# Attention and mixture-of-experts block in fp32: four buffer pairs for pair 1's rotation, and another order of batch 1's preparation

## The chip, the cores and the metric

The kernel runs on one core of a Trainium2 chip. The core has TensorE (PE) for matrix products, VectorE (DVE), ScalarE (ACT) and GpSimd (POOL) for the work on elements, SyncE (SP) to issue most DMAs, an on-chip memory (SBUF) and eight accumulation banks of 128 x 512 fp32 (PSUM), which GpSimd cannot reach. Each engine runs its own instructions in program order and waits on semaphores for the others. The metric is the device time of one launch in microseconds; the median of a few runs counts.

## The reference

The block has two batches of 1024 tokens with 128 features. Modulations (shift, scale, gate, twice) come from a small product. Then attention with 16 heads of 64, with latents of 64 for queries and for keys and values, and a mixture of 8 experts with the two best of each token:

```python
h = _layernorm(x) * (1 + ca) + sa
# inside the attention: a second layer norm with ln_scale, ln_bias
c_q, c_kv = h @ w_down_q.T, h @ w_down_kv.T        # 64 latents each
q, k, v = c_q @ w_up_q.T, c_kv @ w_up_k.T, c_kv @ w_up_v.T
q, k = rope(q), rope(k)                            # rotation by cos and sin
out = softmax(q @ k.T * scale) @ v @ w_out.T + residual
x = x + ga * out
h = _layernorm(x) * (1 + cb) + sb
x = x + gb * moe(h)        # where(weight > 0, relu(h*w @ w1 + b1) @ w2 + b2, out)
```

The attention scores are computed to nearly full fp32 from a rounded upper part (`_hi`) and a remainder (`_lo`) of q and k.

## The kernel before, in words

The work on attention goes by pairs of heads: 8 pairs in each batch, 16 in all, pair 0 to 7 for batch 0. A pair needs its up projections (`up`, q and k with a swapped twin for the rotation), their rotation, their upper and lower parts, the maxima of the scores' rows (16 steps, `maxima` on TensorE and `reduce_max` on VectorE), and then the main loop's 16 score steps with exponentials (ScalarE), values times probabilities (`pv`) and sums of probabilities (`add`, GpSimd). The main loop runs over p = 0 to 15 and 8 groups g of two score steps; beside pair p's scores, group g holds two maxima of pair p+1 and one of the eight units of pair p+2's up projections. So when the loop begins, pair 0 must be complete with maxima, pair 1 rotated, and batch 0 in latents. This is the prologue, where the change lies.

In the prologue, TensorE does batch 0's transposes and latents, `up(0, 0)` to `up(0, 3)`, `up(1, 0)` and `up(1, 1)`, and then the 16 maxima of pair 0. Between them stand `up(1, 2)` and `up(1, 3)`, batch 1's transposes (`transposed(2)`, `transposed(3)`: four tiles each), its latents (`latent(4)` to `latent(7)`) and its values (`values(1)`). Maxima use two pairs of banks in turn, so `maxima(0, n)` waits until the reduction of step n - 2 is done (`max_reduced` at n - 1). The first maxima of pair 1, `maxima(1, 0)`, open the main loop: they wait for all 16 reductions of pair 0.

Pair 1 is rotated on GpSimd: ScalarE copies a unit and its swapped twin out of PSUM (`up_copy(u)`, L727 and L728) to a buffer pair `turn_a`, `turn_b`; GpSimd multiplies both and adds (`turn_1`, L914 to L917); ScalarE writes the upper part (`upper_1`, L734), and GpSimd the lower part (`lower_1`, L923). There are two buffer pairs, so `up_copy(2)` waits for `lower_1(0)` and `up_copy(3)` for `lower_1(1)`.

Batch 1's first steps run along the same engines: ScalarE normalises x (`normalised(h0, x_sb, 0)`, L654, 8 tiles) once VectorE's `inverse(T1, 3)` has given the shifts (L1035); GpSimd modulates (`modulate`, L892, 2 instructions), and stands in front of `turn_1(0)`; VectorE takes the statistics (in program order behind `reduce_max(0, 1)`) and the inverse root (behind `reduce_max(0, 3)`, `shift` at L1035); ScalarE normalises again into `hn`; TensorE transposes, ScalarE scales (`features`, L672), TensorE computes the latents (L377), and ScalarE reads them (`latent_upper`, L680 and L682). GpSimd's last instructions of the prologue are `split(2)` (up weights), `lower_1(3)`, `gated(0)` (L871) and `residual(0, 0)` (L879). The first `add` follows.

SyncE issues eight small DMAs for each half of pair 0's maxima (`max_rows`) once `neg_max` is done; `score(0, 0)` waits for the first half's. The first exponential has a table load before it (L702). After the loop come the last outputs and the experts' products, with gathers and scatters by slots.

Of the kernel before, what the change touches and what calls it, by code (L numbers as in the profile page):

```python
# [10 lines left out]
F32 = mybir.dt.float32  # L11
# [10 lines left out]
HALF = 512  # L22
# [24 lines left out]
def build(nc, t, out):  # L47
    ctx = ExitStack()
    with ctx:
# [10 lines left out]
        x_sb = sb("x_sb", [P, NT, D])  # L60
        h0 = sb("h0", [P, NT, D])
# [58 lines left out]
        turn_a = [hid_sb[:, n, :] for n in range(2)]  # L120
        turn_b = [h2T[:, n * HALF:(n + 1) * HALF] for n in range(2)]
# [224 lines left out]
        def _(pe):  # L346
# [146 lines left out]
            for n in range(NMAX):  # L493
                maxima(0, n)
                if n == 1:
                    up(1, 2)
                    up(1, 3)
                if n == 4:
                    pe.wait_ge(s["up_copied"], 3)
                    transposed(2)  # L500
                    transposed(3)
                if n == 6:
                    pe.wait_ge(s["features"], 4)
                    latent(4)
                    latent(5)
                if n == 8:
                    pe.wait_ge(s["up_copied"], 4)
                    latent(6)
                    latent(7)
                if n == 11:  # L510
                    pe.wait_ge(s["latent_copied"], 2)
                    values(1)
# [121 lines left out]
        def _(act):  # L634
# [86 lines left out]
            def up_copy(u):  # L721

                act.wait_ge(s["up_product"], n_unit(1, u))
                if u >= 2:
                    act.wait_ge(s["pool_lower"], u - 1)
                straight, swapped = unit_banks(1, u)
                nc.scalar.copy(turn_a[u % 2], straight)  # L727
                nc.scalar.copy(turn_b[u % 2], swapped).then_inc(s["up_copied"], 1)  # L728

            def upper_1(u):  # L730
# [3 lines left out]
                nc.scalar.copy(hi_of[w][:, 1, c], turn_a[u % 2]).then_inc(s["pool_upper"], 1)  # L734

            root(3)
            values_out(0)
# [3 lines left out]
            normalised(h0, x_sb, 0).then_inc(s["norm1"], 1)  # L741
# [3 lines left out]
            upper(0, 3)  # L745
            upper_1(0)
            upper_1(1)
            up_copy(2)
            root(4)
            normalised(hn, h0, 1)  # L750
            features(2)
            features(3)
            up_copy(3)
# [75 lines left out]
        def _(pool):  # L829
# [77 lines left out]
            def turn_1(u):  # L907

                w, c = unit_columns(1, u)
                a, b = turn_a[u % 2], turn_b[u % 2]  # L910
# [8 lines left out]
            def lower_1(u):  # L919
# [3 lines left out]
                V.tensor_tensor(lo_of[w][:, 1, c], turn_a[u % 2], hi_of[w][:, 1, c].bitcast(F32),  # L923
# [640 lines left out]
```

## Time and profile before

| | |
|---|---|
| median of 3 runs | 905.26 us (905.06 to 907.29) |
| the profiled execution | 913.83 us |
| its span in the trace | 911.8 us |
| TensorE matmul busy | 818.4 us (90%) |
| GpSimd busy | 663.3 us (73%) |
| VectorE busy | 636.7 us (70%) |
| ScalarE busy | 396.9 us (44%) |
| mean granted TensorE clock | 0.948 |

Times in the trace are microseconds from the span's start. The prologue ends, and the main loop begins, with the first maxima that are written to `ps_m`, at 73.69 us. A row of a timeline merges equal instructions that follow one another: the second number is the time from the first's start to the last's end, and the count of matmuls is higher than that of the program's instructions, since an fp32 product is made in more than one pass. In brackets stands the idle time before, with the engine that ended it. The granted clock is 1.00 at 2.4 GHz and 0.50 at 1.2 GHz.

### The profile page before, as it was taken

How to read it: one execution, taken by the hardware profiler on the slowest of the kernel's cores; microseconds unless marked ns; L12 is line 12 of the kernel's file. 1: busy time of each engine (PE TensorE's matmuls, PEld its weight loads, DVE VectorE, ACT ScalarE, POOL GpSimd, SP SyncE). 2: the span in 40 equal slices, each digit the busy share in tenths (PEclk: the TensorE clock that was granted, in tenths of full speed). 3: DMA queues.
4: the chain of work that ended last, by engine and by line, in shares of the span. 5: the costliest groups of instructions: out<-in, count | busy, mean ns of one | idle time of the engine just before them, and what ended most of it. 6: DMA issues, size and time to landing. Idle time of an engine off the chain costs nothing.

```text
span 911.8 us, 14689 instructions
## 1 busy us (share of the span) xinstructions
PE 818.4 (90%) x5118; PEld 490.1 (54%) x5118; DVE 636.7 (70%) x1156; ACT 396.9 (44%) x650; POOL 663.3 (73%) x348
## 2 busy tenths in 40 slices
PE   4668999999999999999999999999999977788671
PEld 2435555555555555555555555555555443377661
DVE  8957777777777777777777777777776757654112
ACT  3453544444444444444444444444444322345331
POOL 2386998989897878787878787878778845623323
PEclk8968999999999999999999999999999987979786
DMA  9000001010101010101011110101000000186763
GB/s 245 27 1 12 13 13 25 14 25 13 25 13 25 14 25 13 25 13 25 13 27 26 21 25 14 25 13 14 13 14 14 13 13 12 43 267 228 255 228 87
DMA packets 84329, 43.89 MB, mean 48 GB/s; under 512 B 57632, under 2 KB 73376, under 8 KB 84192
## 3 DMA queue, kind: packets, MB, share of 16 engines
q1 hardware_dynamic: 83232, 40.86, 17.6%
q0 software_dynamic: 1024, 2.10, 0.7%
q8 instruction: 41, 0.67, 0.3%
q14 instruction: 32, 0.26, 0.1%
HBM read 36.51 MB, written 6.16 MB: 47 GB/s over the span
## 4 chain that ended last, share of the span: by engine, by line
PE 80%; DVE 8%; issue 4%; POOL 3%; DMA 3%; ACT 1%; SPq 1%; another core or an unknown queue 0%; POOLq 0%; DVEq 0%; ACTq 0%
PE ps_o L456 25%; PE ps_m L422 9%; PE ps_x L410 8%; PE ps_s L440 7%; PE ps_s L446 6%; PE ps_s L442 6%; PE ps_s L444 6%; PE ps_s L473 3%; PE ps_s L464 3%; PE ps_s L591 2%; DMA moe<-xs_dram 2%; PE ps_s L600 1%; DVE mx L1104 1%; POOL xs_dram L960 1%; DVE hn L1193 1%
## 5 line engine op out<-in xcount | busy, mean ns | idle before, releaser
L946 POOL TENSOR_TENSOR acc<-acc,probs 128x1024 f32<-128x1024 f32 (+1 forms) x192 | 459.8, 2395 | 76.2 <-ACT probs L702 53.8
L1104 DVE TENSOR_REDUCE mx<-ps_m 128x2 f32<-128x1024 f32 x240 | 293.7, 1224 | 93.1 <-PE ps_m L422 92.6
L702 ACT ACTIVATE probs<-ps_s 128x1024 f32<-128x1024 f32 x256 | 248.9, 1024 | 163.2 <-PE ps_s L446 163.1
L456 PE MATMUL ps_o<-probs,c_all 128*64 128x512 f32 x1024 | 250.4, 610 | 0.0
L946 POOL TENSOR_TENSOR acc<-probs 128x1024 f32<-128x1024 f32 (+1 forms) x32 | 75.4, 2358 | 54.8 <-ACT probs L702 54.3
L440 PE MATMUL ps_s<-q_hi,k_hi 64*128 64x512 f32 x512 | 103.4, 400 | 12.0 <-DVE x_sb L1160 10.9
L456 PEld LDWEIGHTS ps_o<-probs,c_all 128*64 128x64 f32 x1024 | 62.6, 137 | 93.9 <-issue 44.6
L422 PE MATMUL ps_m<-k_hi,q_hi 64*128 64x512 f32 x480 | 108.0, 445 | 3.9 <-DVE mx L1104 3.9
L442 PE MATMUL ps_s<-q_hi,k_lo 64*128 64x512 f32 x512 | 101.8, 393 | 0.0
L446 PE MATMUL ps_s<-neg_row,one_row 64*128 64x512 f32 x512 | 101.7, 393 | 0.0
L444 PE MATMUL ps_s<-q_lo,k_hi 64*128 64x512 f32 x512 | 101.1, 391 | 0.0
L422 PEld LDWEIGHTS ps_m<-k_hi,q_hi 64*128 64x128 f32 x480 | 46.2, 184 | 90.8 <-issue 80.4
L440 PEld LDWEIGHTS ps_s<-q_hi,k_hi 64*128 64x128 f32 x512 | 49.0, 187 | 24.4 <-issue 17.2
L1160 DVE TENSOR_TENSOR x_sb<-x_sb,ps_s 128x512 f32<-128x512 f32 x30 | 20.6, 686 | 49.9 <-PE ps_s L473 49.9
L444 PEld LDWEIGHTS ps_s<-q_lo,k_hi 64*128 64x128 f32 x512 | 48.9, 187 | 11.1
L442 PEld LDWEIGHTS ps_s<-q_hi,k_lo 64*128 64x128 f32 x512 | 49.1, 187 | 10.7
L446 PEld LDWEIGHTS ps_s<-neg_row,one_row 64*128 64x128 f32 x512 | 48.8, 186 | 10.9
L714 ACT COPY den<-ps_s 128x512 f32<-128x512 f32 x30 | 17.6, 585 | 78.0 <-PE ps_s L464 78.0
L1091 DVE TENSOR_TENSOR ps_x<-ps_x,tmp 128x256 f32<-128x256 f32 x112 | 48.4, 432 | 3.8
L694 ACT CAST q_hi<-ps_x 128x256 fp32r<-128x256 f32 x56 | 20.9, 374 | 66.6 <-DVE ps_x L1091 66.6
L1086 DVE TENSOR_TENSOR ps_x<-ps_x,rot 128x256 f32<-128x256 f32 x112 | 47.3, 422 | 0.0
L1089 DVE TENSOR_TENSOR tmp<-ps_x,rot 128x256 f32<-128x256 f32 (+1 forms) x113 | 47.0, 416 | 0.0
(289 smaller groups left out, 1030.5 us busy)
## 6 DMA issues: line engine op xcount, KB each, us to landing
probs<-in_experts SPq DMA_DIRECT2D x15, 578.0 KB
rr<-rd_dram SPq DMA_DIRECT2D x62, 128.0 KB
wu<-in_wqk SPq DMA_DIRECT2D x16, 256.0 KB, 3.2
neg_row<-nm SPq DMA_DIRECT2D x256, 0.5 KB, 2.0
w_first<-in_experts SPq DMA_DIRECT2D x5, 578.0 KB
rot<-in_experts SPq DMA_DIRECT2D x5, 578.0 KB
hT<-in_experts SPq DMA_DIRECT2D x5, 578.0 KB
xs_dram<-zero SPq DMA_DIRECT2D x2, 960.0 KB, 7.4
```

The lines of the kernel that those rows point to most:

```text
L410: ins = nc.tensor.matmul(bank, m[:, q % 2, w, twin, :], src, start=(n == 0), stop=(n == 1))
L422: ins = nc.tensor.matmul(bank[:, h, :], q_hi[rows(h), q % 3, qt * P:(qt + 1) * P], k_hi[rows(h), q % 3, kh * HALF:(kh + 1) * HALF], start= ...
L440: nc.tensor.matmul(bank[h], k_hi[rows(h), p % 3, kc], q_hi[rows(h), p % 3, qc], start=True, stop=False)
L442: nc.tensor.matmul(bank[h], k_lo[rows(h), p % 3, kc], q_hi[rows(h), p % 3, qc], start=False, stop=False)
L444: nc.tensor.matmul(bank[h], k_hi[rows(h), p % 3, kc], q_lo[rows(h), p % 3, qc], start=False, stop=False)
L446: ins = nc.tensor.matmul(bank[h], one_row[rows(h), :], neg_row[rows(h), p % 2, qc], start=False, stop=True)
L456: ins = nc.tensor.matmul(ps_o[64 * h:64 * h + 64, :], c_all[:, (p // HP) * TB + kt, :], probs[:, st % 4, h, :], start=(kt == 0), stop=(kt ...
L702: nc.scalar.activation(probs[:, st % 4, :, :], ps_s[:, 2 * (st % 2):2 * (st % 2) + 2, :], ACT.Exp, scale=SCALE).then_inc(s["probs"], 1)
L946: V.tensor_tensor(acc[:, half, heads, :], first, probs[:, st % 4, heads, :], ALU.add).then_inc(s["added"], 1)
L1086: V.tensor_tensor(straight, straight, cos_sb[:, c], ALU.mult).then_inc(s["turned"], 1)
L1091: V.tensor_tensor(straight, straight, part, ALU.add).then_inc(s["rotated"], 1)
L1104: V.reduce_max(mx[:, :, kh, qt], max_banks(q, n), AX.X).then_inc(s["max_reduced"], 1)
```

## The change

It has three parts. First, `turn_a` and `turn_b` get two more members each, in `rr` and in the second half of `acc`, and each unit of pair 1 has its own buffer pair; the wait of `up_copy` on `pool_lower` is gone. Second, ScalarE's order: the first normalisation of batch 1 stands ahead of `values_out(0)`, `up_copy(2)` and `up_copy(3)` follow `upper(0, 3)`, and `upper_1(1)` stands behind the second normalisation. Third, TensorE's order between the maxima: `transposed(2)` and `transposed(3)` go behind steps 6 and 7 instead of both behind step 4; the four latents go one by one behind steps 9 to 12 instead of two by two behind steps 6 and 8; `values(1)` goes behind step 14 instead of 11. No instruction is added or taken away on any engine.

```diff
--- before.py
+++ after.py
@@ -117,8 +117,8 @@
         wo_sb = p_flat[0:64, 0:H * D].rearrange("p (h d) -> p h d", h=H)
         g_tmp, g_abs = [probs[:, 2 + n, 0, :].rearrange("p (b m d) -> p b m d", b=B, m=2) for n in range(2)]
         g_raw = w_first[:, 0:HP * D]
-        turn_a = [hid_sb[:, n, :] for n in range(2)]
-        turn_b = [h2T[:, n * HALF:(n + 1) * HALF] for n in range(2)]
+        turn_a = [hid_sb[:, n, :] for n in range(2)] + [rr[:, 0, :], acc[:, 1, 0, :]]
+        turn_b = [h2T[:, n * HALF:(n + 1) * HALF] for n in range(2)] + [rr[:, 1, :], acc[:, 1, 1, :]]
 
         latent_raw = [moe[:].rearrange("p a d -> p (a d)")[64:128, n * HALF:(n + 1) * HALF] for n in range(3)]
         latent_raw.append(rt_sb[:].rearrange("p a d -> p (a d)")[64:128, 0:HALF])
@@ -495,19 +495,14 @@
                 if n == 1:
                     up(1, 2)
                     up(1, 3)
-                if n == 4:
+                if n in (6, 7):
                     pe.wait_ge(s["up_copied"], 3)
-                    transposed(2)
-                    transposed(3)
-                if n == 6:
+                    transposed(n - 4)
+                if n >= 9 and n < 13:
                     pe.wait_ge(s["features"], 4)
-                    latent(4)
-                    latent(5)
-                if n == 8:
                     pe.wait_ge(s["up_copied"], 4)
-                    latent(6)
-                    latent(7)
-                if n == 11:
+                    latent(n - 5)
+                if n == 14:
                     pe.wait_ge(s["latent_copied"], 2)
                     values(1)
             pe.wait_ge(s["values"], 2)
@@ -721,36 +716,34 @@
             def up_copy(u):
 
                 act.wait_ge(s["up_product"], n_unit(1, u))
-                if u >= 2:
-                    act.wait_ge(s["pool_lower"], u - 1)
                 straight, swapped = unit_banks(1, u)
-                nc.scalar.copy(turn_a[u % 2], straight)
-                nc.scalar.copy(turn_b[u % 2], swapped).then_inc(s["up_copied"], 1)
+                nc.scalar.copy(turn_a[u], straight)
+                nc.scalar.copy(turn_b[u], swapped).then_inc(s["up_copied"], 1)
 
             def upper_1(u):
 
                 w, c = unit_columns(1, u)
                 act.wait_ge(s["pool_rotated"], u + 1)
-                nc.scalar.copy(hi_of[w][:, 1, c], turn_a[u % 2]).then_inc(s["pool_upper"], 1)
+                nc.scalar.copy(hi_of[w][:, 1, c], turn_a[u]).then_inc(s["pool_upper"], 1)
 
             root(3)
+            normalised(h0, x_sb, 0).then_inc(s["norm1"], 1)
             values_out(0)
             folded_out()
             upper(0, 0)
             upper(0, 1)
-            normalised(h0, x_sb, 0).then_inc(s["norm1"], 1)
             up_copy(0)
             upper(0, 2)
             up_copy(1)
             upper(0, 3)
+            up_copy(2)
+            up_copy(3)
             upper_1(0)
-            upper_1(1)
-            up_copy(2)
             root(4)
             normalised(hn, h0, 1)
+            upper_1(1)
             features(2)
             features(3)
-            up_copy(3)
             upper_1(2)
             for n in range(4, 8):
                 latent_upper(n)
@@ -907,7 +900,7 @@
             def turn_1(u):
 
                 w, c = unit_columns(1, u)
-                a, b = turn_a[u % 2], turn_b[u % 2]
+                a, b = turn_a[u], turn_b[u]
                 if u == 0:
                     pool.wait_ge(rot_in, 32)
                 pool.wait_ge(s["up_copied"], u + 1)
@@ -920,7 +913,7 @@
 
                 w, c = unit_columns(1, u)
                 pool.wait_ge(s["pool_upper"], u + 1)
-                V.tensor_tensor(lo_of[w][:, 1, c], turn_a[u % 2], hi_of[w][:, 1, c].bitcast(F32),
+                V.tensor_tensor(lo_of[w][:, 1, c], turn_a[u], hi_of[w][:, 1, c].bitcast(F32),
                                 ALU.subtract).then_inc(s["pool_lower"], 1)
 
             turn_1(0)
```

On TensorE, the rows from behind `up(1, 3)` to batch 1's values stand as follows before (L422 are the maxima, L370 the transposes, L377 the latents, L384 the values):

```order
L422 MATMUL ps_s<-k_hi,q_hi 128x512 x6
L370 MATMUL ps_m<-ident,hn 128x128 x8
L422 MATMUL ps_s<-k_hi,q_hi 128x512 x4
L377 MATMUL ps_m<-hT,wd_sb 128x512 x2
L422 MATMUL ps_s<-k_hi,q_hi 128x512 x4
L377 MATMUL ps_o<-hT,wd_sb 128x512
L377 MATMUL ps_x<-hT,wd_sb 128x512
L422 MATMUL ps_s<-k_hi,q_hi 128x512 x6
L384 MATMUL ps_m<-wd_sb,hT 128x64 x8
L422 MATMUL ps_s<-k_hi,q_hi 128x512 x8
```

and after the change, up to the last latent but not the two maxima and the values behind it:

```order
L422 MATMUL ps_s<-k_hi,q_hi 128x512 x10
L370 MATMUL ps_m<-ident,hn 128x128 x4
L422 MATMUL ps_s<-k_hi,q_hi 128x512 x2
L370 MATMUL ps_m<-ident,hn 128x128 x4
L422 MATMUL ps_s<-k_hi,q_hi 128x512 x4
L377 MATMUL ps_m<-hT,wd_sb 128x512
L422 MATMUL ps_s<-k_hi,q_hi 128x512 x2
L377 MATMUL ps_m<-hT,wd_sb 128x512
L422 MATMUL ps_s<-k_hi,q_hi 128x512 x2
L377 MATMUL ps_o<-hT,wd_sb 128x512
L422 MATMUL ps_s<-k_hi,q_hi 128x512 x2
L377 MATMUL ps_x<-hT,wd_sb 128x512
```

Here the transposes are parted and later by two and three steps of maxima, and each latent has two matmuls of one maxima step on either side.

On ScalarE, from the root that opens batch 1's chain (`sd`), the rows stand as follows before (L654 `h0` is the first normalisation, L686 `values_out`, L666 `folded_out`, L694 the upper parts of pair 0, L727 and L728 `up_copy`):

```order
L642 ACTIVATE sd<-sd 128x8
L686 COPY c_all<-ps_m 128x512
L666 COPY w_first<-ps_m 128x512
L666 COPY w_first<-ps_o 128x512
L694 CAST k_hi<-ps_s 128x512
L694 CAST q_hi<-ps_s 128x512
L654 ACTIVATE h0<-x_sb,shift,sd 128x128 x8
L727 COPY hid_sb<-ps_s 128x512
L728 COPY h2T<-ps_s 128x512
L694 CAST k_hi<-ps_m 128x512
L727 COPY hid_sb<-ps_s 128x512
L728 COPY h2T<-ps_s 128x512
```

and after the change (the same instructions have line numbers lower by 5 to 7):

```order
L637 ACTIVATE sd<-sd 128x8
L649 ACTIVATE h0<-x_sb,shift,sd 128x128 x8
L681 COPY c_all<-ps_m 128x512
L661 COPY w_first<-ps_m 128x512
L661 COPY w_first<-ps_o 128x512
L689 CAST k_hi<-ps_s 128x512
L689 CAST q_hi<-ps_s 128x512
L720 COPY hid_sb<-ps_s 128x512
L721 COPY h2T<-ps_s 128x512
L689 CAST k_hi<-ps_m 128x512
L720 COPY hid_sb<-ps_s 128x512
L721 COPY h2T<-ps_s 128x512
```

The first normalisation has moved from behind `q_hi` of unit 1 to the place ahead of `c_all`; what followed it keeps its order.

Next on ScalarE, from the upper part of pair 0's last unit (L694 `q_hi<-ps_o`) to the upper part of pair 1's unit 2 (`k_hi`), the rows stand as follows before:

```order
L694 CAST q_hi<-ps_o 128x512
L734 CAST k_hi<-hid_sb 128x512
L734 CAST q_hi<-hid_sb 128x512
L727 COPY hid_sb<-ps_m 128x512
L728 COPY h2T<-ps_m 128x512
L642 ACTIVATE sd<-sd 128x8
L654 ACTIVATE hn<-h0,shift,sd 128x128 x8
L672 ACTIVATE hT<-ps_m,lns 128x512 x2
L727 COPY hid_sb<-ps_o 128x512
L728 COPY h2T<-ps_x 128x512
L734 CAST k_hi<-hid_sb 128x512
```

and after the change:

```order
L689 CAST q_hi<-ps_o 128x512
L720 COPY rr<-ps_m 128x512
L721 COPY rr<-ps_m 128x512
L720 COPY acc<-ps_o 128x512
L721 COPY acc<-ps_x 128x512
L727 CAST k_hi<-hid_sb 128x512
L637 ACTIVATE sd<-sd 128x8
L649 ACTIVATE hn<-h0,shift,sd 128x128 x8
L727 CAST q_hi<-hid_sb 128x512
L667 ACTIVATE hT<-ps_m,lns 128x512 x2
L727 CAST k_hi<-rr 128x512
```

The copies of units 2 and 3 now go to `rr` and `acc` ahead of the first `upper_1`, and `upper_1(1)` (`q_hi<-hid_sb`) comes behind the eight tiles of `hn`. GpSimd's order is unchanged.

## Rows read from the trace of the kernel before

**Rows 1.** The page's chain that ended last: share of the span by engine.
```profile
PE 80%; DVE 8%; issue 4%; POOL 3%; DMA 3%; ACT 1%; SPq 1%; another core or an unknown queue 0%; POOLq 0%; DVEq 0%; ACTq 0%
```
**Rows 2.** Busy time of each engine by window, inside the main loop.
```profile
200.00:400.00 200.00, 200.00 (x1270) 113.82 (x1270) 154.29 (x253) 93.06 (x128) 171.19 (x77) 1.00 0.10 19
```
**Rows 3.** Timeline of ScalarE: start, us, line, operation, count, idle before and releaser.
```profile
29.59 0.58 ACT L686 COPY c_all<-ps_m 128x512 f32<-128x512 f32 x1 [4.62 <-PE ps_m L384]
...
33.10 3.19 ACT L654 ACTIVATE h<-x_sb,shift,sd 128x128 f32<-128x128 f32 x8
...
36.66 0.59 ACT L728 COPY h2T<-ps_s 128x512 f32<-128x512 f32 x1
...
52.57 3.19 ACT L654 ACTIVATE hn<-h,shift,sd 128x128 f32<-128x128 f32 x8 [1.29 <-DVE shift L1035]
```
**Rows 4.** Timeline of GpSimd (POOL) in the prologue.
```profile
36.37 4.85 POOL L892 TENSOR_TENSOR h<-h,mod 128x1024 f32<-128x1024 f32 x2 [14.19 <-ACT h L654]
...
41.18 1.26 POOL L914 TENSOR_TENSOR hid_sb<-hid_sb,rot 128x512 f32<-128x512 f32 x1
...
48.75 1.26 POOL L923 TENSOR_TENSOR k_lo<-hid_sb,k_hi 128x512 fp32r<-128x512 f32 x1
...
51.25 1.26 POOL L914 TENSOR_TENSOR hid_sb<-hid_sb,rot 128x512 f32<-128x512 f32 x1 [1.24 <-ACT h2T L728]
...
70.08 2.35 POOL L879 TENSOR_TENSOR h<-h,mod 128x1024 f32<-128x1024 f32 x1
```
**Rows 5.** Timeline of VectorE (DVE) in the prologue.
```profile
25.86 0.17 DVE L1035 SCALAR_TENSOR_TENSOR shift<-mv,sd 128x8 f32<-128x8 f32 x1
...
39.81 2.35 DVE L1104 TENSOR_REDUCE mx<-ps_s 128x2 f32<-128x1024 f32 x2
...
44.95 2.34 DVE L1104 TENSOR_REDUCE mx<-ps_s 128x2 f32<-128x1024 f32 x2
...
51.55 0.99 DVE L1035 SCALAR_TENSOR_TENSOR shift<-mv,sd 128x8 f32<-128x8 f32 x1
...
68.93 4.62 DVE L1104 TENSOR_REDUCE mx<-ps_s 128x2 f32<-128x1024 f32 x4 [0.79 <-PE ps_s L422]
```
**Rows 6.** Timeline of TensorE (PE) from pair 1's projections to the loop's third group.
```profile
34.83 0.39 PE L410 MATMUL ps_s<-ck,wl 128*128 128x512 f32 x1
...
46.31 0.80 PE L422 MATMUL ps_s<-k_hi,q_hi 64*128 64x512 f32 x2 [3.51 <-DVE mx L1104]
...
53.21 3.07 PE L370 MATMUL ps_m<-ident,hn 128*128 128x128 f32 x8 [6.10 <-ACT hn L654]
...
56.22 1.22 PE L422 MATMUL ps_s<-k_hi,q_hi 64*128 64x512 f32 x4
...
57.37 3.78 PE L377 MATMUL ps_m<-hT,wd_sb 128*128 128x512 f32 x4
...
62.19 1.12 PE L377 MATMUL ps_o<-hT,wd_sb 128*128 128x512 f32 x2
...
66.45 2.00 PE L384 MATMUL ps_m<-wd_sb,hT 128*128 128x64 f32 x16
...
73.69 0.80 PE L422 MATMUL ps_m<-k_hi,q_hi 64*128 64x512 f32 x2 [1.76 <-DVE mx L1104]
...
84.95 0.50 PE L422 MATMUL ps_m<-k_hi,q_hi 64*128 64x512 f32 x2
```
**Rows 7.** Windows of 1 us with the granted clock (PEclk) where it changes.
```profile
45.00:46.00 1.00, 0.00 (x0) 0.00 (x0) 1.00 (x2) 0.62 (x1) 1.00 (x2) 0.51 0.00 0
...
62.00:63.00 1.00, 1.00 (x4) 0.49 (x3) 1.00 (x1) 0.37 (x1) 1.00 (x1) 0.95 0.00 0
...
72.00:73.00 1.00, 0.00 (x0) 0.00 (x0) 1.00 (x2) 0.00 (x0) 0.43 (x1) 0.67 0.00 0
...
79.00:80.00 1.00, 0.66 (x5) 0.48 (x5) 1.00 (x3) 0.00 (x0) 0.96 (x1) 0.92 0.08 1
```
**Rows 8.** Waits in the last 111 us: engine, line, releaser: us, times, longest.
```profile
ACT hid_sb L797 <- remote: 9.4, 2, 6.8
```

## The prediction

> **What bounds the kernel now.** I read the page's chain first: TensorE carries 80% of it [rows 1]. The windows say why: from 200 to 400 us TensorE is busy for 200.00 of 200.00 us, GpSimd for 171 and VectorE for 154 [rows 2]. In the loop TensorE's order is the limit, and none of its instructions changes there. So the question is when `maxima(1, 0)`, the loop's first instruction, starts: 73.69 us now, behind VectorE's last reduction of pair 0 [rows 6]. What the prologue gains there is carried to the end, as long as the loop has no slack to swallow it; with TensorE gapless it has none.
>
> Then the timelines of the prologue, engine by engine. The reader is to see a relay: ScalarE's first normalisation of batch 1 starts at 33.10, though its shifts were there at 26.03 [rows 3, 5]; ScalarE instead waited 4.62 us for `values_out` [rows 3]. GpSimd waits 14.19 us for it and modulates from 36.37 [rows 4]. `turn_1(0)` follows at 41.18, and `lower_1(0)` ends at 50.0; only then does `up_copy(2)` run, because it needs the buffer; behind it stand the root and the second normalisation, which starts at 52.57 [rows 3, 4]. VectorE had its statistics by 44.95 [rows 5]. TensorE waits 6.10 us for `hn` [rows 6], with the granted clock down to half speed since 45 us [rows 7], so that transposes, latents and maxima from 53.21 to 62 run at 1.2 GHz.
>
> **First half of the change: the start of the chain.** The normalisation now begins at 26.1 and takes 3.19 us, to 29.3. `values_out` was released at 29.59 [rows 3], so the gap of 4.62 us holds it and costs it nothing; the cover is thin, 0.3 us, and every 0.1 us above that would delay `values_out`, the folded weights and `up(0, 2)` by as much. GpSimd's two modulations (4.85 us, rows 4) run from 29.4 to 34.2. `up_copy(0)` no longer stands behind the normalisation, but it needs `up(1, 0)`, whose last matmul ends at 35.2 [rows 6]; its two copies end at 36.4, against 37.25 before [rows 3]. So `turn_1(0)` starts at 36.4 and not at 41.18: 4.8 us earlier. A `turn_1` is 3.8 us (41.18 to 44.97) and a `lower_1` 1.26 us [rows 4].
>
> The first maxima move little: `up(1, 1)` cannot be earlier, since it waits for VectorE. VectorE starts its first two reductions at 39.7, against 39.81 [rows 5], and the statistics end at 44.9 as now.
>
> **Four buffer pairs.** `up_copy(2)` and `up_copy(3)` run as their products appear, at 40.3 and 41.3, when ScalarE has nothing else to do. They cost the path nothing. What they buy is that the root and the second normalisation no longer stand behind `lower_1(0)`. What is late next is VectorE's order: reductions 2 and 3 stand in front of the inverse root and end at 47.2 [rows 5]. The root itself (ScalarE, 0.2 us) is done by 45.4. Then the inverse and the shift: 0.2 us, and 0.99 us for the shift beside a busy GpSimd, against 0.17 us for the same instruction with GpSimd idle [rows 5]. GpSimd will be busy at that time too (`turn_1(2)`), so I take 0.99. The normalisation then starts at 48.6 and ends at 51.8, against 52.57 and 55.76 [rows 3]: 4.0 us earlier.
>
> A page of the Trainium skill bears on this shift: "GPSIMD Engine Reference", section 1 (Specifications), says that GpSimd shares its SBUF interfaces with VectorE and that they contend when VectorE's instruction has two SBUF inputs or runs in a two-port mode. The row at 51.55 agrees and has the size that the page lacks. With the contention-free 0.17 us everything behind the shift would come 0.8 us sooner; the sum goes by the row.
>
> `upper_1(1)` now waits behind these eight tiles, to 52.3, so `lower_1(1)` on GpSimd starts at 52.4, though GpSimd was free at 49.0. Behind it: `turn_1(3)` to 57.4, `lower_1(2)` to 58.7, `split(2)` to 61.2. The added wait of about 3 us is GpSimd's alone, and I follow it below.
>
> **TensorE between the maxima.** `maxima(4)` and `maxima(5)` follow reductions 2 and 3, cold (0.80 us, rows 6). Reduction 4 runs from 48.5 to 49.7, behind the shift; `maxima(6)` from 49.8. From here TensorE has work without a gap. At 1.2 GHz a maxima step is 0.6 us (1.22 for two), four transposes 1.53 (3.07 for eight), a latent 1.87 (3.78 for two); at 2.4 GHz a maxima step is 0.45 and a latent 1.0 (1.12 with the rise inside it) [rows 6]. In order: maxima 6 to 50.4, transposes to 51.9, maxima 7 to 52.5, transposes to 54.0 (the last tile is ready at 51.8), maxima 8 and 9 to 55.2, latent 4 (features ready at 54.9) to 57.1, maxima 10 to 57.7, latent 5 to 59.5.
>
> When does the clock rise? Today TensorE's unbroken work begins at 53.21 and the rise comes at 62.05 [rows 6, 7], 8.8 us later and 5.8 us after the last transpose. The same two distances from 50.4 and 54.0 give 59.2 and 59.8; I take 59.5. Then maxima 11 to 60.0, latent 6 to 61.0, maxima 12 to 61.5, latent 7 to 62.5, maxima 13 and 14 to 63.5, values (2.00 us, rows 6) to 65.4, maxima 15 to 65.9, and its reduction to 67.2 (four take 4.62 us, rows 5; one alone 1.2). VectorE is not behind: its reductions 8 to 14 need 1.2 us each and each gets its banks 1.5 us or more apart, but for the last three, of which reduction 14 ends at 65.5. Moving the values from step 11 to 14 costs some 0.6 us here, since reduction 15 now waits for them; it is in the sum. The loop begins at 67.3 instead of 73.69: 6.4 us.
>
> Bounds for the unseen clock: if it stays at half speed through all pieces, latents 6 and 7 end at 62.0 and 64.5, the values at 67.6, and the loop begins at 69.6: 4.1 us. If it rises at 55.2, the loop begins at 65.4: 8.3 us.
>
> **The loop's first groups.** Today the clock falls again at 72.67, after 69.1 to 72.7 in which TensorE had only short maxima between four reductions [rows 5, 7], and the first groups run at 1.2 GHz to 79.1. Groups 0 and 1 take 11.26 us, 73.69 to 84.95 [rows 6]. In the new order latents and values fill the place in front of the loop, and the longest gap there is 1.4 us, the last reduction. I expect the clock to stay at 2.4 GHz. Then 5.4 us of cold work could shrink by 2.7 at the most; walking through groups 0 and 1, `maxima(1, 2)` and `maxima(1, 3)` still wait for reductions of 1.24 us and the two rotations on VectorE, and I get 9.2 us: 2.0 saved. The bounds are 0 and 2.7.
>
> **GpSimd at the loop's start.** Latent 7 is read by ScalarE to 63.8 (two copies of 0.58, as in rows 3), `upper_1(3)` to 64.4, `lower_1(3)` to 65.7, `gated(0)` to 68.1, `residual(0, 0)` (2.35 us, rows 4) to 70.4. The first `add` needs the probabilities of step 1, at 70.9 with a warm clock. So GpSimd is just in time, and its wait for `upper_1(1)` is covered; without this cover it would eat into a slack of (200 - 171)/200, about 0.7 us in each group of 5.03. The maximum rows leave SyncE at 53.9, land by 61, and are early. The table load of the exponential falls behind `values_out(1)`, from 66 to 67.3, ahead of its first use at 68.7.
>
> The sum: 6.4 + 2.0 = 8.4 us. The profiled execution would be 913.83 - 8.4 = 905.4 us, the median 905.26 - 8.4 = 896.9 us. The median runs stand 8.6 us below the profiled one; the gapless loop makes the prologue's gain the same in both, so I subtract and do not scale.
>
> **Rivals.** (a) The clock falls in front of the loop all the same, or has not risen long enough. For it: it fell at 45 about 2.2 us after the last matmul, and at 72.67 although work was scattered over the time before. Against: the gap is shorter and the work before it denser. Then 6.4 us alone: 898.9. (b) The clock stays low up to the loop: 4.1 us, 901.2. For it: there is one rise of this kind in the rows, and no other to tell how far it varies. (c) The clock rises early: 8.3 + 2.0 = 10.3 us, 894.9. (d) The head start is swallowed: GpSimd late by its chain `upper_1(1)`, `lower_1(1)` to `residual(0, 0)`, so that the exponentials wait for `add`. It would take back at most what GpSimd is late; from 70.4 to 78.6, 8 us of delay, nothing would be left: 905.3. Against: GpSimd has waited 3 us once and nothing else. (e) Slower: the experts' part at the end has waits that no instruction of the kernel ends, 9.4 us in two of them for ScalarE [rows 8]. If the code of an engine arrives late there, the time is lost on the path. The profiled execution, 8.6 us above the median, may be such a case. The changed program has the same instructions in other places; with 9.4 us more than today's median runs have, it would give 906.3. It decides from 8.4 us on. Against it: nothing in the change is near that part, and three runs lie within 2.3 us.
>
> **How the numbers follow.** The forecast has 0.58, (a) 0.18, (b) 0.06, (c) 0.10, (d) 0.04, (e) 0.04. The forecast's own range is 895.3 to 898.3, from 0.8 us for the shift and 0.7 us either way for the loop's first groups. The range of 8 in 10 goes from 894.2, below (c), to 901.3, which takes in (a) and (b). A change under 0.3% (2.7 us) can't be told from none. Faster means under 902.5: the forecast, (a), (b) and (c), with one hundredth off for a smaller sum: 0.91. The same: 0.05, (d) and that hundredth. Slower: 0.04.
>
> **What would show it.** In the profile after: ScalarE's `h` tiles end before 29.5 and `c_all` keeps its start at 29.6; GpSimd's modulation starts at 29.4, `turn_1(0)` at 36.4; `hn` starts at 48.6; the first `maxima` on `ps_m` is at 67.3; the granted clock rises near 59.5 and is 1.00 at 68 to 72; groups 0 and 1 last 9.2 us. The forecast is wrong if `hn` waits for something else than the shift, if the clock is 0.50 at the loop's start, if GpSimd's first `add` comes after the probabilities that it adds, or if TensorE shows gaps between 100 and 690 us that are not there now.

## The result, and the profile after

The changed kernel takes 897.46 us in the median of 5 runs (895.69 to 899.75), against 905.26 before: a ratio of 0.9908, 95% interval 0.9885 to 0.9930. The forecast was 896.9. A second series (below) gave 0.9925 (0.9898 to 0.9951). The profiled execution took 895.69 us with a span of 894.0.

ScalarE's timeline after (start, us, line, operation, count, idle before and releaser) answers to [rows 3]:

```profile
25.98 3.19 ACT L649 ACTIVATE h<-x_sb,shift,sd 128x128 f32<-128x128 f32 x8 [1.09 <-DVE shift L1028]
29.49 0.58 ACT L681 COPY c_all<-ps_m 128x512 f32<-128x512 f32 x1 [0.32 <-PE ps_m L384]
...
47.91 3.19 ACT L649 ACTIVATE hn<-h,shift,sd 128x128 f32<-128x128 f32 x8 [2.36 <-DVE shift L1028]
```

The first normalisation fills the gap, 0.32 us of it is left, and `c_all` keeps its start. `hn` starts at 47.91 (48.6 forecast) and is released by the shift.

GpSimd's timeline after answers to [rows 4]:

```profile
29.25 4.87 POOL L885 TENSOR_TENSOR h<-h,mod 128x1024 f32<-128x1024 f32 x2 [6.72 <-ACT h L649]
36.35 1.29 POOL L907 TENSOR_TENSOR hid_sb<-hid_sb,rot 128x512 f32<-128x512 f32 x1 [2.23 <-ACT h2T L721]
...
51.69 1.26 POOL L916 TENSOR_TENSOR q_lo<-hid_sb,q_hi 128x512 fp32r<-128x512 f32 x1 [2.62 <-ACT q_hi L727]
...
66.26 2.42 POOL L872 TENSOR_TENSOR h<-h,mod 128x1024 f32<-128x1024 f32 x1
68.83 2.39 POOL L939 TENSOR_TENSOR acc<-probs 128x1024 f32<-128x1024 f32 x1 [0.15 <-ACT probs L697]
```

`turn_1(0)` starts at 36.35, `lower_1(1)` has waited for `upper_1(1)`, and the first `add` comes 0.15 us after the residual's end, released by ScalarE: just in time, as worked out.

TensorE's timeline after answers to [rows 6]:

```profile
46.59 0.79 PE L422 MATMUL ps_s<-k_hi,q_hi 64*128 64x512 f32 x2 [4.17 <-DVE mx L1097]
47.72 0.80 PE L422 MATMUL ps_s<-k_hi,q_hi 64*128 64x512 f32 x2 [0.34 <-DVE mx L1097]
49.16 0.80 PE L422 MATMUL ps_s<-k_hi,q_hi 64*128 64x512 f32 x2 [0.65 <-DVE mx L1097]
49.89 1.11 PE L370 MATMUL ps_m<-ident,hn 128*128 128x128 f32 x4
...
53.87 2.07 PE L377 MATMUL ps_m<-hT,wd_sb 128*128 128x512 f32 x2
...
61.50 2.00 PE L384 MATMUL ps_m<-wd_sb,hT 128*128 128x64 f32 x16
63.43 0.50 PE L422 MATMUL ps_s<-k_hi,q_hi 64*128 64x512 f32 x2
65.35 0.50 PE L422 MATMUL ps_m<-k_hi,q_hi 64*128 64x512 f32 x2 [1.42 <-DVE mx L1097]
...
74.54 0.50 PE L422 MATMUL ps_m<-k_hi,q_hi 64*128 64x512 f32 x2
```

The 6.10 us wait for `hn` is gone; the loop starts at 65.35 instead of 73.69, and groups 0 and 1 take 9.19 us (74.54 - 65.35) instead of 11.26. The granted clock (third number from the right) rose early and did not fall again before the third group:

```profile
56.00:57.00 1.00, 1.00 (x3) 0.46 (x4) 0.29 (x1) 0.98 (x2) 1.00 (x2) 0.68 0.08 1
...
65.00:66.00 1.00, 0.65 (x6) 0.66 (x8) 0.49 (x3) 0.42 (x1) 1.00 (x1) 1.00 0.00 0
```

So in this pair of traces the third group starts 10.4 us earlier, more than the 8.4 forecast, while the medians moved 7.8.

### The profile page after: what moved, and what is told of

Its sections match the earlier page's. It is cut to its first block, busy times and chain, and to the rows that moved or that the text cites. A ratio compares the mean times of both kernels' runs of the same rounds, so it can differ in the third digit from the quotient of the medians.

```text
span 894.0 us, 14690 instructions
## 1 busy us (share of the span) xinstructions
PE 813.2 (91%) x5118; PEld 485.9 (54%) x5118; DVE 637.1 (71%) x1156; ACT 397.2 (44%) x650; POOL 662.7 (74%) x348
## 4 chain that ended last, share of the span: by engine, by line
PE 82%; DVE 8%; DMA 4%; POOL 2%; issue 2%; ACT 1%; POOLq 0%; SPq 0%; DVEq 0%
PE ps_o L456 25%; PE ps_m L422 9%; PE ps_x L410 8%; PE ps_s L440 7%; PE ps_s L442 6%; PE ps_s L446 6%; PE ps_s L444 6%; PE ps_s L473 3%; DMA moe<-xs_dram 3%; PE ps_s L464 3%; PE ps_s L595 2%; PE ps_s L586 2%; POOL xs_dram L953 2%; DVE mx L1097 1%; PE ps_s L377 1%
## 5 line engine op out<-in xcount | busy, mean ns | idle before, releaser
L422 PE MATMUL ps_m<-k_hi,q_hi 64*128 64x512 f32 x480 | 107.7, 444 | 4.0 <-DVE mx L1097 4.0
L939 POOL TENSOR_TENSOR acc<-probs 128x1024 f32<-128x1024 f32 (+1 forms) x32 | 75.4, 2357 | 48.3 <-ACT probs L697 47.8
L422 PEld LDWEIGHTS ps_m<-k_hi,q_hi 64*128 64x128 f32 x480 | 46.0, 183 | 91.4 <-issue 81.3
L440 PEld LDWEIGHTS ps_s<-q_hi,k_hi 64*128 64x128 f32 x512 | 48.7, 186 | 24.0 <-issue 17.0
L1153 DVE TENSOR_TENSOR x_sb<-x_sb,ps_s 128x512 f32<-128x512 f32 x30 | 20.6, 685 | 49.9 <-PE ps_s L473 49.9
L444 PEld LDWEIGHTS ps_s<-q_lo,k_hi 64*128 64x128 f32 x512 | 48.7, 186 | 10.8
L446 PEld LDWEIGHTS ps_s<-neg_row,one_row 64*128 64x128 f32 x512 | 48.6, 185 | 10.8
L442 PEld LDWEIGHTS ps_s<-q_hi,k_lo 64*128 64x128 f32 x512 | 48.7, 186 | 10.5
L709 ACT COPY den<-ps_s 128x512 f32<-128x512 f32 x30 | 17.6, 585 | 77.9 <-PE ps_s L464 77.9
```

The source lines that it names most:

```text
L422: ins = nc.tensor.matmul(bank[:, h, :], q_hi[rows(h), q % 3, qt * P:(qt + 1) * P], k_hi[rows(h), q % 3, kh * HALF:(kh + 1) * HALF], start= ...
L440: nc.tensor.matmul(bank[h], k_hi[rows(h), p % 3, kc], q_hi[rows(h), p % 3, qc], start=True, stop=False)
L442: nc.tensor.matmul(bank[h], k_lo[rows(h), p % 3, kc], q_hi[rows(h), p % 3, qc], start=False, stop=False)
L444: nc.tensor.matmul(bank[h], k_hi[rows(h), p % 3, kc], q_lo[rows(h), p % 3, qc], start=False, stop=False)
L446: ins = nc.tensor.matmul(bank[h], one_row[rows(h), :], neg_row[rows(h), p % 2, qc], start=False, stop=True)
L939: V.tensor_tensor(acc[:, half, heads, :], first, probs[:, st % 4, heads, :], ALU.add).then_inc(s["added"], 1)
```

## The experiments

Each row is one trace, with the median of its own series; the changed kernel has four traces. Since the traces are up to 1.9 us apart by the time of this step, I count from VectorE's first `shift` row (25.86 before, 25.78 after). The columns: start of ScalarE's `hn`, of the loop and of the third group (all from that shift), the clock in the first two groups ("low" is low at their start), the median and the ratio to the kernel before in the same series.

| kernel | `hn` | loop | third group | clock in groups 0, 1 | median us | ratio (95%) |
|---|---|---|---|---|---|---|
| before | 26.7 | 47.8 | 59.1 | low | 905.26 |  |
| before_again | 26.8 | 47.7 | 58.2 | low | 905.88 | 1.0006 (0.9995 to 1.0016) |
| changed | 22.1 | 39.6 | 48.8 | high | 897.46 | 0.9908 (0.9885 to 0.9930) |
| after_again | 21.0 | 38.4 | 47.6 | high | 899.20 | 0.9925 (0.9898 to 0.9951) |
| after_third | 21.0 | 38.5 | 47.7 | high | (894.55, one) |  |
| after_fourth | 23.6 | 40.1 | 50.9 | falls | (896.44, one) |  |
| pe_order_only | 26.8 | 45.6 | 54.8 | high | 902.79 | 0.9978 (0.9963 to 0.9994) |
| scalar_only | 22.2 | 43.4 | 54.0 | low | 902.62 | 0.9972 (0.9955 to 0.9989) |
| norm_late | 23.1 | 39.9 | 50.6 | falls | 898.01 | 0.9905 (0.9882 to 0.9928) |
| two_buffers | 22.2 | 41.2 | 50.4 | high | 897.42 | 0.9918 (0.9888 to 0.9948) |
| before_warm | 26.7 | 50.7 | 60.2 | rises at once | 907.14 | 1.0008 (0.9989 to 1.0026) |
| after_warm | 22.1 | 37.8 | 48.5 | falls | 897.96 | 0.9917 (0.9885 to 0.9949) |
| warm_all | 21.0 | 39.4 | 48.6 | high | 896.99 | 0.9899 (0.9883 to 0.9914) |
| warm_fit | 23.6 | 38.9 | 48.1 | high | 897.14 | 0.9894 (0.9873 to 0.9915) |

**The two kernels once more.** No edit.

> The kernel before once more, unchanged, for a second trace. Theory: the waits of ScalarE and VectorE in the experts' part that no instruction ends (about 17 us summed over the engines in the first trace, and none in the changed kernel's) are not a property of either kernel; here they are absent or elsewhere, and the profiled time is near 905. Rival: they belong to this kernel and come back, with a profiled time near 914, and then a part of the gain comes from the placement of code. The loop's start is at 73.7 us, within 1 us by either.

> The changed kernel once more, unchanged. Theory: the loop's start lies between 65 and 69.6 us, according to when TensorE's granted clock rises between 56 and 60 us, and the first two groups take 9.2 us; the rest of the spread sits in the experts' part. Rival: the loop's start is the same to 0.3 us each time and the whole spread comes from the experts' part. Median expected 897.5 us.

In `before_again` the profiled time is 904.02 us and the waits that no instruction ends [rows 8] are absent, so they belong to one execution and not to the kernel; rival (e) did not come. The changed kernel's loop start moved by 1.1 us (38.4 against 39.6), neither by 4 nor by 0.3, so both sides of that expectation were off. The 1.1 us is a small VectorE instruction: `sd<-mv` (L1021) took 1.29 us in the first trace and 0.17 in the second (last section). Over the four traces `hn` starts 21.0 to 23.6 us behind the first shift.

**TensorE's order alone; ScalarE's order and buffers alone.**

```diff
 # pe_order_only = before with the new placement between the maxima:
-                if n == 4: transposed(2), transposed(3)
-                if n == 6: latent(4), latent(5)
-                if n == 8: latent(6), latent(7)
-                if n == 11: values(1)
+                if n in (6, 7): transposed(n - 4)
+                if n >= 9 and n < 13: latent(n - 5)
+                if n == 14: values(1)
 # scalar_only = after with these lines the other way round
```

> The kernel before with TensorE's new order alone (transposes behind steps 6 and 7, latents behind 9 to 12, values behind 14). Theory: hn still starts at 52.6; from maxima 6 on it goes as in the changed kernel (49.2 to 65.4, 16.2 us), but from 53.6, so the loop starts at 69.8 and with a warm clock: 3.9 + 2.0 = 5.9 us gained, median about 899.4. Rival: the order only pays with the earlier hn; alone it costs what the values' move costs, and the gain is under 2 us (over 903).

> The changed kernel with TensorE's order of before: four buffer pairs and ScalarE's order alone. Theory: hn starts at 47.9, as in the changed kernel; the transposes then hold reductions 5 and 6, and the last four maxima run alone at the end, so the loop starts at 69.4 with the clock falling again: 4.3 us gained, median about 901.0. Rival: it is the earlier hn that brings the whole gain, and the order of TensorE nothing: 65.4 to 66 for the loop's start and 897 to 898 in the median.

In the medians the order alone gave 2.4 us, not 5.9; ScalarE's part alone 2.6, not 4.3. In `pe_order_only` maxima 6 started at 53.69, as expected, but the loop began at 71.32 instead of 69.8:

```profile
53.69 0.80 PE L422 MATMUL ps_s<-k_hi,q_hi 64*128 64x512 f32 x2 [5.60 <-DVE mx L1099]
...
59.17 2.04 PE L377 MATMUL ps_m<-hT,wd_sb 128*128 128x512 f32 x2 [0.71 <-issue]
...
61.87 1.85 PE L377 MATMUL ps_m<-hT,wd_sb 128*128 128x512 f32 x2
63.64 0.50 PE L422 MATMUL ps_s<-k_hi,q_hi 64*128 64x512 f32 x2
...
71.32 0.49 PE L422 MATMUL ps_m<-k_hi,q_hi 64*128 64x512 f32 x2 [1.42 <-DVE mx L1099]
```

From maxima 6 to the loop it takes 17.6 us, and not the 16.2 of the changed kernel. Two things make up the 1.4 us. Latent 4 stands still for 0.71 us until `up_copy(3)` has ended at 59.07, since this kernel has two buffer pairs and the changed kernel has no such wait. And the clock rose only at 63.4, so that latent 5 took 1.85 us instead of 1.13.

In `scalar_only` the loop starts where it was expected (43.4 from the shift, against 69.4 - 25.8 = 43.6). The clock falls at 61.1, during the values (59.96 to 62.64) and ahead of the last four maxima, and the groups cost 10.65 us.

The table shows which part gives what. ScalarE's part brings `hn` 4.6 us forward and leaves the way from `hn` to the third group as it was (31.9 us, against 32.4 and 31.4 before). The order leaves `hn` where it was and shortens this way to 28.1; with both it is 26.6, 26.6, 26.6 and 27.3. So the third group comes 3.8 and 4.6 us earlier with one part and 9.9 with both. That is nearly a sum: the 1.5 us above it is about what `pe_order_only` lost to the wait for `up_copy(3)` and the late rise. The medians say the same, 2.4 and 2.6 against 6.0 in the same series, and their intervals don't separate 5.0 from 6.0. Why these two medians gained 1.4 and 2.0 us less than their traces is open. The three moves within TensorE's order (transposes, latents, values) were not run apart.

**What brings `hn` forward.** `norm_late` moves the first normalisation back; `two_buffers` keeps it early and takes two of the four buffer pairs away.

```diff
 # norm_late
-            normalised(h0, x_sb, 0).then_inc(s["norm1"], 1)
             values_out(0)
...
             upper(0, 1)
+            normalised(h0, x_sb, 0).then_inc(s["norm1"], 1)
             up_copy(0)
 # two_buffers
-        turn_a = [...] + [rr[:, 0, :], acc[:, 1, 0, :]]      (and turn_b)
+                if u >= 2: act.wait_ge(s["pool_lower"], u - 1)
-            up_copy(2), up_copy(3), upper_1(0), root(4), normalised(hn, h0, 1), upper_1(1), features(2), features(3)
+            upper_1(0), upper_1(1), up_copy(2), root(4), normalised(hn, h0, 1), features(2), features(3), up_copy(3)
```

> The changed kernel with batch 1's first normalisation back behind upper(0, 1). Theory A (VectorE's order is the gate of hn): the statistics stand behind reduction 1 and end at 45 whether the modulation ends at 34 or at 41, so hn starts where it does in the changed kernel (47.9, within 0.5), and only GpSimd is 4.8 us later, which its waits cover to within 0.5 us at the first add: the loop starts at 65.4 (at the same clock) and the median is that of the changed kernel, 897.5 to 899.2. Theory B (the prediction's relay: ScalarE's early start is what brings the gain): hn at 51 to 52.6 and a median of 902 or more.

> The changed kernel with two buffer pairs, and ScalarE's order of before behind upper(0, 3), but with the early normalisation and TensorE's new order. Theory A: with GpSimd 4.8 us earlier, lower_1(0) ends at 45.3 and up_copy(2) at 46.3, so hn still starts at the shift, 47.9; up_copy(3) ends at 54.7 and holds latent 4 by 0.8 us at most; the loop starts at 65.4 to 66.2, median within 1 us of the changed kernel's. Theory B (the four buffers are needed): hn later than 50 and a median of 901 or more.

Theory A holds in both medians, 898.01 and 897.42; no difference from the changed kernel can be measured. The rows of VectorE, then ScalarE, of `norm_late` show it, though GpSimd's modulation ended 7 us later than in the changed kernel:

```profile
40.47 2.35 DVE L1097 TENSOR_REDUCE mx<-ps_s 128x2 f32<-128x1024 f32 x2
42.74 1.64 DVE L1015 BATCH_NORM_STATS2 bst<-h 128x6 f32<-128x128 f32 x8
...
46.19 2.34 DVE L1097 TENSOR_REDUCE mx<-ps_s 128x2 f32<-128x1024 f32 x2
48.46 0.18 DVE L1026 RECIPROCAL sd<-sd 128x8 f32<-128x8 f32 x1
48.67 0.17 DVE L1028 SCALAR_TENSOR_TENSOR shift<-mv,sd 128x8 f32<-128x8 f32 x1
```

```profile
48.88 3.19 ACT L649 ACTIVATE hn<-h,shift,sd 128x128 f32<-128x128 f32 x8 [2.36 <-DVE shift L1028]
```

VectorE goes from reduction to statistics to reductions to the shift without a gap: its own order gates `hn`, whichever of the two edits is made. `hn` is 1.0 us later than in the changed kernel's first trace, twice my tolerance, since the first reductions started 1.0 us later (40.47 against 39.42). Of this, 0.66 us comes from a wait of VectorE for TensorE at 33.3. It is not the edit's: the granted clock was 0.50 there until 35.8 in this execution, as in `before_again` and `after_fourth`, whose VectorE waited 1.01 and 0.97 us at the same place, and 1.00 in the first traces. The other 0.4 is the price of the normalisation in front of `up_copy`, which holds the first maxima. Counted from the first shift, 23.1 lies within the changed kernel's own 21.0 to 23.6.

In `two_buffers`, `hn` starts at 22.2 as in the changed kernel's first trace, but the loop starts 1.6 us later (41.2 against 39.6), where theory A allowed 0.8:

```profile
47.20 3.18 ACT L649 ACTIVATE hn<-h,shift,sd 128x128 f32<-128x128 f32 x8 [1.36 <-DVE shift L1030]
```

```profile
53.94 2.05 PE L377 MATMUL ps_m<-hT,wd_sb 128*128 128x512 f32 x2 [0.71 <-issue]
55.91 0.80 PE L422 MATMUL ps_s<-k_hi,q_hi 64*128 64x512 f32 x2
56.64 1.95 PE L377 MATMUL ps_m<-hT,wd_sb 128*128 128x512 f32 x2
```

Latent 4 waits 0.71 us for `up_copy(3)`, as in `pe_order_only`, and the clock rises at 58.3, so latent 5 takes 1.95 us instead of 1.13. Whether that wait also delays the rise is not shown.

Each of the two edits thus frees the second normalisation on its own, and with neither (`pe_order_only`) more than half of the gain is missing. For `hn` the four buffers and the early normalisation are one gain, not two. The buffers also take away the 0.71 us of latent 4, too little to be seen in a median.

**The clock.** Extra products on TensorE fill waits, to hold the clock.

```diff
+            def filler(count):
+                pe.wait_ge(s["up_copied"], 3); pe.wait_ge(rot_in, 32)
+                for _ in range(count):
+                    nc.tensor.matmul(ps_m[:, 1, 0:QUART], wd_sb[:, 0, :], cos_sb[:, 0:QUART], start=True, stop=True)
             for n in range(NMAX):
                 maxima(0, n)
+                if n in FILL: filler(FILL[n])
 # before_warm: before, FILL = {13: 2, 14: 1, 15: 3}
 # after_warm: after, FILL = {3: 8};  warm_all: {3: 8, 5: 7, 15: 5};  warm_fit: {3: 8, 5: 4, 15: 3}
```

> The kernel before with six extra small products (128x256, their results unused) on TensorE, behind maxima steps 13 (two), 14 (one) and 15 (three), in gaps in which it waits for reductions. They cost nothing where they stand. Theory: the clock then does not fall in front of the loop; the loop starts at 73.7 as before, and groups 0 and 1 take 9.2 us and not 10.5 to 11.3: 1.3 to 2.0 us gained, median about 903.5. Rival: the clock falls all the same, since these gaps are short already, and nothing is gained (905.3 within 0.7).

> The changed kernel with eight extra small products (128x256, results unused) behind maxima step 3, where TensorE waits 4.2 us for reduction 2. Theory: the clock does not fall at 46, so the pieces from 46.6 to 57 run at 2.4 GHz; then reductions at 1.17 us each set the pace from 47.8, and the loop starts at 62.5 to 63.5 instead of 65.4: 2 to 3 us less than the changed kernel, near 895.5, and with less spread from run to run, since no rise has to be waited for. Rival: the clock is not worth anything here because VectorE's reductions are the pace already, and the median stays within 0.7 us.

`before_warm` refutes its own premise. The clock had fallen at 67.5, before the fillers, and they cost twice as much there (three took 2.93 us, against 1.56 in `warm_fit`, where the clock was 1.00):

```profile
69.60 2.07 PE L499 MATMUL ps_m<-rot,wd_sb 128*128 128x256 f32 x4
71.61 0.79 PE L423 MATMUL ps_s<-k_hi,q_hi 64*128 64x512 f32 x2
...
74.20 2.93 PE L499 MATMUL ps_m<-rot,wd_sb 128*128 128x256 f32 x6
77.06 0.79 PE L423 MATMUL ps_m<-k_hi,q_hi 64*128 64x512 f32 x2
```

The maxima behind them are held back and the loop starts 3 us late; a clock that rises at once (groups 0 and 1: 9.50 us) gives 1.0 to 1.8 back. In `after_warm` the early fillers held the clock to 49.9, it rose again at 53.3, and the loop starts at 37.8 from the shift, the earliest of all; but the clock fell at 63.5, 0.2 us in front of the loop, and the third group gained nothing. The median is within 0.7 us of the first series' 897.46, as the rival said, but not for the rival's reason alone, since the clock did not hold.

> The changed kernel with extra small products (128x256, results unused) on TensorE behind maxima step 3 (eight), 5 (seven) and 15 (five), sized to the waits that the traces show at 2.4 GHz (4.2, 2.0 and 1.4 us). Theory: the clock stays at 2.4 GHz from 41 us on and through the loop's start; the loop starts at 62.8 to 63.3 and its first two groups take 9.2 us, so the third group starts near 72.2, 2.3 us ahead of the changed kernel's first trace; median near 895.5. Rival: when the clock is low at the time, the extra products take twice as long, fill more than their gap and delay the maxima behind them, as in the kernel before with extra products, where the loop started at 77.1; then the median is 898 or more and the runs spread over 8 us.

> As the kernel with extra products behind steps 3, 5 and 15, but four instead of seven behind step 5 and three instead of five behind 15, since one of them took 0.465 us and seven lasted 3.3 us in a gap of 2.0. Theory: the clock stays at 2.4 GHz as there, and the maxima are no longer held back: the third group starts 1.5 to 2 us earlier counted from ScalarE's h tiles (46.5 to 47 us behind them against 48.4), and the median is near 895.5, against 905.9 before. Rival: with fewer products the clock falls again at one of the two places, and the median is that of the changed kernel with its spread (897.5 to 899).

In both, the clock was 1.00 from 41 us on and through the loop. Neither theory's median came (896.99 and 897.14). In `warm_all` the fillers were too long, as the rows show: seven took 3.29 us in a gap of 2, and five in front of the loop 2.42 us, of which some 0.9 held the loop's first maxima:

```profile
46.29 3.29 PE L499 MATMUL ps_m<-rot,wd_sb 128*128 128x256 f32 x14
49.51 0.49 PE L423 MATMUL ps_s<-k_hi,q_hi 64*128 64x512 f32 x2
...
61.69 2.42 PE L499 MATMUL ps_m<-rot,wd_sb 128*128 128x256 f32 x10
64.05 0.50 PE L423 MATMUL ps_m<-k_hi,q_hi 64*128 64x512 f32 x2
```

With fewer of them (`warm_fit`) the clock held as well, and the third group started at 48.1 from the shift instead of 48.6, 0.5 us earlier and not 1.5 to 2. In this trace `sd<-mv` and the second `shift` on VectorE took 0.67 and 1.28 us instead of 0.17 each. From `hn` on, `warm_fit` needs 24.5 us to the third group, against 26.6 in three traces of the changed kernel: the 2 us expected are there in the trace, and the late `hn` hides them. The runs of `warm_all` lie within 1.8 us (895.76 to 897.55), those of `warm_fit` within 5.5, those of the changed kernel within 4 and 8 us. Whether either beats the changed kernel in the median can't be told: the intervals overlap. Nor do they exclude 2 us.

**Two more traces of the changed kernel.** No edit.

> The changed kernel once more, for another trace of the clock. Theory: where the time is 2 us and more above the fastest trace's (893.5 us of span), the traces show why: the clock falls in front of the loop and groups 0 and 1 take 10.5 to 11.3 us instead of 9.2, or the rise comes later than 57 us. Rival: both are as in the first trace, and the difference lies behind 720 us.

> The changed kernel a fourth time, for another trace of the clock, with the same theories as for the third: a start of the third group between 72.3 and 76.5 us, and the rest of the difference between runs in the experts' part.

`after_fourth` shows rival (a) of the prediction at work. The granted clock falls at 65.7, 0.4 us behind the loop's start, and rises at 69.1:

```profile
65.28 0.51 PE L422 MATMUL ps_m<-k_hi,q_hi 64*128 64x512 f32 x2 [1.42 <-DVE mx L1097]
...
70.84 0.50 PE L422 MATMUL ps_m<-k_hi,q_hi 64*128 64x512 f32 x2 [0.74 <-DVE mx L1097]
...
76.06 0.50 PE L422 MATMUL ps_m<-k_hi,q_hi 64*128 64x512 f32 x2
```

Groups 0 and 1 take 10.78 us (76.06 - 65.28) with the same gap of 1.42 us ahead of them. The third group starts at 76.06, within the expected 72.3 to 76.5. `after_third` is as the first traces (9.20 us, clock high). Neither is 2 us above the fastest trace, so the question of the slower runs stays. The four traced executions took 894.55 to 896.44 us, while seven of the nine others lie at 897.46 to 901.71.

## Why the prediction was right, step by step

The direction and the place held. The median came within 0.6 us of the forecast in the first series and within 2.3 in the second, in part by luck, as the end of this section says. By its own steps:

- **The loop carries the gain: nearly.** TensorE is busy for 200.00 of 200.00 us from 200 to 400 after as before. From the third group to VectorE's `hn` tiles near 720 it is 645.6 us before (730.58 - 84.95) and 645.6 to 646.1 in the changed kernel's four traces; up to 0.5 us is given back.
- **ScalarE's gap holds the first normalisation; `turn_1(0)` at 36.4:** 25.98 to 29.2 and 36.35.
- **VectorE's shift gates `hn`:** shown by `norm_late` and `two_buffers`. What the prediction did not say is that either edit alone gets there. By its own times `lower_1(0)` ends at 45.3 once the normalisation is early, so that two buffer pairs would have let `up_copy(2)` and the root go ahead of the shift as well.
- **The shift at 0.99 us:** 0.17 in three of the four traces and 1.27 in the fourth; `sd<-mv`, which the prediction took from one row (0.62), varied in the same way (0.17, 0.17, 0.64 and 1.29). The two together move `hn` by up to 1.6 us from one execution to the next. The forecast's own range counts 0.8 us for the shift both ways, though against 0.99 it could fall by 0.8 and rise by 0.3.
- **TensorE's pieces:** right in order. Four transposes took 1.04 us (49.89 to 50.93), not 1.53, because the row of eight in [rows 6] includes waits for the tiles of `hn`. A maxima step took 0.73 and not 0.6.
- **The clock rises at 59.5:** mis-sized. It rose at 56.6 in the first trace and at 54.2 to 55.5 in the others. The prediction carried over one distance, 8.8 us from the start of unbroken work to the rise. In ten traces without extra products it is 5.5 (`after_fourth`) to 9.9 us (`two_buffers`), and 8.9 and 6.1 in the two of the kernel before; the two longest have the 0.71 us wait of latent 4 inside.
- **The loop at 67.3:** 65.35 in the first trace, 8.3 us earlier than before and not 6.4. That is the value of rival (c), but the rise is the smaller part of it. TensorE was ahead of the forecast by 0.6 us at maxima 6 (49.16 against 49.8) and by 1.3 at latent 4 (53.87 against 55.2), both at the low clock: the shift and the transposes. The rise brought about 0.5 more by the end of latent 5 (57.66 against 59.5), most of it because this latent ran at the high clock.
- **The bound of 4.1 us for a clock that stays low:** too favourable. It has the values at 2.00 us, a row at the high clock; in `scalar_only` they took 2.68 us with the fall inside them. No run shows the whole case.
- **Warm first groups, 9.2 us:** 9.19 or 9.20 in three traces of four; 10.78 in the fourth, where rival (a) came true. The gap in front of the loop was 1.42 us in all of them, so its length does not decide alone, and the prediction's reason was too strong.
- **GpSimd just in time:** 0.15 us of idle between the residual and the first `add`; rival (d) took nothing back. In `norm_late` there were 1.46 us of idle, since the clock fell at 66.5 and the probabilities came later.

Counted from the shift, the third group starts at 58.7 in the mean of two traces before and at 48.7 in the mean of four after: 9.9 us. The medians differ by 6.0 to 7.8. The sum of 8.4 lies between: the transposes, the shift and the rise were sized too small, and against them stands a loss of 2 to 4 us between the traces and the medians that the prediction did not have. That the two nearly cancel is luck. The experts' part lasts 173.1 to 175.1 us after VectorE's `hn` tiles in the four traces and 173.3 in `before_again` (181.2 in the first trace of before, with the waits of [rows 8]), which explains 0.7 us of it in the mean and no more.

The rest stays open, since no trace shows one of the changed kernel's slower runs. The mean granted clock, which is on record for every run, points to time at the low clock. In the second series the three slow runs (900.56 to 901.71) had 0.955 to 0.956, the two fastest 0.958 and 0.961; in `after_warm` the four fastest had 0.960 to 0.962, the run of 905.33 had 0.953. In the first series of five there is no such order. The loop leaves little room for it (clock 1.00 from 90 to 690 us in the first and the fourth trace), the experts' part more (0.89 and 0.87 from 690 to 890 us), but where the slower runs lose their time is not shown.

## What to carry to other kernels

When several edits free the same instruction, look for what is late next on its engine before adding up their gains: here VectorE's program order was next, and two edits bought the same start of `hn`. To see whether two parts of a change need each other, split the time at the instruction between them. Here one part moved `hn` and the other shortened the way from it to the loop, and their gains nearly add up. A distance to the rise of the clock that was read from one trace is not safe to carry over, since it varied by 4 us here. Idle time that is filled to hold the clock must be sized for the low clock too, or it delays what it should help.

## What the runs showed of the hardware

Two VectorE instructions of 8 columns, `shift<-mv,sd` and `sd<-mv`, cost 0.17 us, or up to 1.3 us beside a busy GpSimd, and the rows show when: one that starts within a GpSimd instruction does not end before it. In `after_warm`, first VectorE, then GpSimd:

```profile
46.78 1.21 DVE L1038 SCALAR_TENSOR_TENSOR shift<-mv,sd 128x8 f32<-128x8 f32 x1
```

```profile
46.70 1.27 POOL L918 TENSOR_TENSOR rr<-rr,rot 128x512 f32<-128x512 f32 x1
48.05 1.26 POOL L920 TENSOR_TENSOR rr<-rr 128x512 f32<-128x512 f32 x1
```

Started 0.08 us into GpSimd's 1.27 us, it ends at 47.99, with GpSimd's (47.97). In the changed kernel's first trace `shift` began at 47.71, as one of GpSimd's instructions ended, and took 0.17; `sd<-mv` at 44.02 took 1.29 and ended at 45.31, GpSimd's at 45.28. The reciprocal of the same 8 columns is not held: in the kernel before it took 0.20 us at 51.31, within GpSimd's instruction of 51.25 to 52.51. The Trainium skill, "GPSIMD Engine Reference", section 1 (Specifications), names the contention for the form of `shift` (two inputs from SBUF); the size, a wait to the end of the other's instruction, is from these rows. VectorE's rotations read PSUM and one SBUF input, and kept 0.68 to 0.70 us beside GpSimd's modulation, which the change moved onto them.
